# Twelve-stage perceiver decoder: weight-load commands, barriers and small preparations at the seams between stages

## What is computed

```python
x = x + L0_xattn(ln(x), ctx)         # joint attention over own and context tokens
x = x + L0_attn(ln(x))               # self attention, decay, gate
x = x + L0_ffn(ln(x))                # 8 experts, top 2, and a shared one
x = x + L1_xattn(ln(x), ctx, mask)   # 6 decoder layers: self, cross, MLP, each with a norm behind it
x = x + L1_attn(ln(x))
x = x + L1_ffn(ln(x))                # 8 experts, top 2
x = x + L2_xattn(ctx, ctx, ln(x), mask)   # attention at sampled positions
x = x + L2_attn(ln(x))               # cos and sin features (Fourier)
x = x + L2_ffn(ln(x))                # silu(gate) * up, then down; int weights times 1/127
x = x + L3_xattn(ln(x), ctx)
x = x + L3_attn(ln(x))               # gated recurrence
x = x + L3_ffn(ln(x))                # self attention, softplus(temperature) in the queries
return x
```

## Time and profile before

| | |
|---|---|
| median of three runs | 4102.86 us |
| the profiled execution: its own time | 4100.83 us |
| its span, first to last instruction | 4099.0 us |
| mean granted TensorE clock | 0.943 |
| busy: PE, DVE, ACT, POOL | 90%, 63%, 43%, 20% |
| decoder stage, first to last instruction | 690.9 to 2561.2 us |
| DMA | 334.49 MB, mean 82 GB/s |

### The profile page before, as it was taken

How to read it: one execution, slowest core, us unless ns; L and a number is a source line. 1 busy time by engine, 2 the same in 40 slices (tenths; PEclk the granted TensorE clock), 3 DMA queues, 4 the chain that set the end, 5 groups by cost and what they waited for, 6 DMA issues and landing times. The chain is left out here.

```text
span 4099.0 us, 98863 instructions
## 1 busy us (share of the span) xinstructions
PE 3673.6 (90%) x40620; PEld 2808.6 (69%) x40620; DVE 2571.7 (63%) x5495; ACT 1757.3 (43%) x4869; POOL 821.9 (20%) x1040
## 2 busy tenths in 40 slices
PE   7997996999999999999999998759689979888766
PEld 5775985677777777777777776548556679555435
DVE  4445213688888888888888885641168857355545
ACT  1221321444445444444444444312167736266523
POOL 1111101222222222222222222120121100012200
PEclk9998998999999999999999999869889979999877
DMA  4222486001101111101111100227655410010001
GB/s 170 94 81 76 159 301 221 32 32 44 63 32 44 63 33 54 53 33 54 53 38 49 58 28 2 62 86 280 241 185 179 156 37 1 28 42 22 12 7 57
DMA packets 141790, 334.49 MB, mean 82 GB/s; under 512 B 31320, under 2 KB 92184, under 8 KB 122912
## 3 DMA queue, kind: packets, MB, share of 16 engines
q1 hardware_dynamic: 138272, 319.76, 22.9%
q0 software_dynamic: 3072, 8.39, 0.6%
HBM read 301.62 MB, written 26.48 MB: 80 GB/s over the span
## 5 line engine op out<-in xcount | busy, mean ns | idle before, releaser
L2613 POOL TENSOR_TENSOR layers_probs<-layers_probs,layers_rates 128x512 f32<-128x512 f32 x384 | 399.9, 1063 | 867.7 <-DVE layers_rates L2536 867.7
L2640 ACT COPY layers_pT<-banks 128x512 f32<-128x512 f32 x384 | 226.1, 589 | 478.8 <-PE banks L2441 478.8
L2676 ACT ACTIVATE layers_probs<-banks,layers_negmax 128x256 f32<-128x256 f32 x768 | 354.4, 478 | 85.2 <-DVE layers_negmax L2528 85.2
L2370 PE MATMUL banks<-ctx_tiles,weights_a 128*128 128x512 f32 x768 | 364.3, 597 | 0.0
L2377 PE MATMUL banks<-weights_a,ctx_tiles 128*128 128x256 f32 x1536 | 363.1, 379 | 0.0
L2377 PEld LDWEIGHTS banks<-weights_a,ctx_tiles 128*128 128x128 f32 x1536 | 284.6, 190 | 75.9 <-issue 46.1
L2441 PE MATMUL banks<-const,layers_probs 128*128 128x128 f32 x1536 | 243.8, 282 | 3.0 <-POOL layers_probs L2613 3.0
L2441 PEld LDWEIGHTS banks<-const,layers_probs 128*128 128x128 f32 x1536 | 172.3, 142 | 106.6 <-issue 78.6
L2527 DVE TENSOR_REDUCE layers_negmax<-banks 128x4 f32<-128x1024 f32 x192 | 233.7, 1217 | 4.1 <-PE banks L2434 1.6
L2502 DVE COPY layers_V<-banks 128x512 f32<-128x512 f32 x192 | 132.4, 690 | 107.7 <-PE banks L2377 97.7
L2653 ACT ACTIVATE layers_KT<-banks,layers_key_bias 128x512 f32<-128x512 f32 x192 | 133.1, 693 | 155.0 <-PE banks L2370 154.8
(11 more groups left out here) (703 smaller groups left out, 8152.5 us busy)
## 6 DMA issues: line engine op xcount, KB each, us to landing
ctx_tiles<-ctx_rel SPq DMA_DIRECT2D x56, 1024.0 KB, 5.5
weights_a<-in_L_w SPq DMA_DIRECT2D x46, 1024.0 KB, 5.4
l2x_B<-positions SPq DMA_DIRECT2D x32, 1280.0 KB, 6.0
weights_b<-in_L_w SPq DMA_DIRECT2D x32, 1024.0 KB, 6.2
weights_c<-in_L_w SPq DMA_DIRECT2D x16, 1024.0 KB, 7.1
weights_b<-in_L_xattn_w SPq DMA_DIRECT2D x12, 1024.0 KB, 7.4
ctx_tiles<-in_ctx SPq DMA_DIRECT2D x8, 1028.0 KB, 5.7
l0x_key_rows<-in_ctx_rows SPq DMA_DIRECT2D x32, 256.0 KB, 2.7
```

Source lines behind the costliest of these rows:

```text
L2370: last = mm(o, ca_wk[:, c, m * P:(m + 1) * P], E.ctx[:, tile % 2, c, 2 * i * KW:2 * (i + 1) * KW], start=c == 0, stop=c == DC - 1)
L2613: nc.gpsimd.tensor_tensor(probs[:, cc, j // 2, at], probs[:, cc, j // 2, at], rates[:, cc, j // 2, at].unsqueeze(2).to_broadcast([P, 2, KW ...
L2640: nc.scalar.copy(pT[:, k % 4].rearrange("p t c x -> p (t c x)"), o).then_inc(s["evac_act"], 1)
L2676: a(probs[:, cc, j // 2, r], ps[:, r, 0:KW], ACT.Exp, bias=negmax[:, cc, j // 2, r:r + 1], accum_out=totals[:, cc, j // 2, r:r + 1]).then_ ...
```

## The change

1. `end_round` can leave its barrier out. It does so where `await_weights` follows directly: at the end of all twelve stages (after l3f, where the program ends). The small Blocks that stay (`fill` of "proj", `prepare_decay`, `feature_major`, `prepare_centred`) keep theirs.
2. `await_weights` takes several names with one barrier; three pairs are joined.
3. `send_for` moves from the seam into SP's program of the next Block, as `begin` (first thing in l0a, l1a, Fourier and the gated MLP; after step 1 in the decoder; in l2x after the first seven key loads).
4. The fill Blocks of `floor` and `half_pi` go: the one memset moves into `prepare_decay`, the other into the first fill.
5. The decoder's sum goes from one instruction behind the stage to one a tile, behind the last layer's norm.
6. The integer weights are turned in six pieces of 128x768 on DVE inside the Fourier stage, after `mask(k)` at r = 2 of tiles 2 to 7. Their loads are issued at the start of that stage.
7. Softplus moves into `prepare_centred`, on DVE and ACT, ahead of what waits for PE there, with one table load instead of two.
8. The output is stored by eight DMAs of 128 KB at the end of l3f, each when its tile's sum is done.

```diff
-def end_round(nc, handles):
+def end_round(nc, handles, barrier=True):
...
-    nc.all_engine_barrier(sem_only=True)
+    if barrier:
+        nc.all_engine_barrier(sem_only=True)
...
-def await_weights(E, name):
+def await_weights(E, *names):
-    sem, n = E.loads[name]
-    E.nc.sync.wait_ge(sem, 16 * n)
-    E.nc.sync.sem_clear(sem)
+    for name in names:
+        sem, n = E.loads[name]
+        E.nc.sync.wait_ge(sem, 16 * n)
+        E.nc.sync.sem_clear(sem)
     E.nc.all_engine_barrier(sem_only=True)
...
-                        link(v.tensor_tensor(E.x[:, GB * i + g], E.x[:, GB * i + g], y, ALU.add))
+                        v.tensor_tensor(E.x[:, GB * i + g], E.x[:, GB * i + g], y, ALU.add).then_inc(s["x_done"], 1)
...
             def _(sp):
+                if begin:
+                    begin()
                 for g in range(NG):
...
+                if out is not None:
+                    for g in range(NG):
+                        sp.wait_ge(s["x_done"], g + 1)
+                        sp.dma_start(out[:, g], E.x[:, g]).then_inc(s["out_stored"], 16)
+                    sp.wait_ge(s["out_stored"], 16 * NG)
...
                         sp.dma_start(E.ctx[:, step % 2, :, 0:GB * KW], E.ctx_rel[step % NG]).then_inc(s[f"ctx{step % 2}"], 16)
+                    if step == 1:
+                        begin()
...
                     v.tensor_tensor(E.h[:, tile], y, LN_ROWS[kind][:, 2], ALU.add).then_inc(s["h_" + kind], 1)
+                    if kind == "dm":
+                        summed[0] += 1
+                        if summed[0] > (NL - 1) * NG:
+                            dve.wait_ge(s["h_dm"], summed[0])
+                            link(v.tensor_tensor(E.x[:, tile], E.x[:, tile], E.h[:, tile], ALU.add))
...
-                nc.vector.tensor_tensor(E.x[:], E.x[:], E.h[:], ALU.add).then_inc(t["added"], 1)
...
+                v.scalar_tensor_tensor(a[:], E.col("temperature"), -1.0, E.col("temperature"), ALU.mult, ALU.max).then_inc(s["abs"], 1)
+                link(v.tensor_scalar(softplus[:], E.col("temperature"), 0.0, None, ALU.max))
+                dve.wait_ge(s["ln"], 1)
+                link(v.tensor_tensor(softplus[:], softplus[:], a[:], ALU.add))
                 dve.wait_ge(s["done"], 1)
...
                     sp.wait_ge(s["job_done"], number["KV", (K - 4, 1)] + 1)
                     load_ctx(K)
+                begin()
                 for it in range(T):
...
+                def dequantise(piece):
+                    if piece == 0:
+                        sem, n = E.loads[ints_name]
+                        dve.wait_ge(sem, 16 * n)
+                    dst, src = ints[piece // 2]
+                    half = src.shape[1] // 2
+                    at = slice(piece % 2 * half, (piece % 2 + 1) * half)
+                    v.tensor_scalar(dst[:, at], src[:, at], float(np.float32(1.0 / 127.0)), None, ALU.mult).then_inc(s["dequantised"], 1)
...
+                    if r == 2 and g >= 2:
+                        dequantise(g - 2)
...
-        await_weights(E, "L0x")
-        await_weights(E, "L0a")
+        await_weights(E, "L0x", "L0a")
...
-        await_weights(E, "L0f")
-        await_weights(E, "later")
+        await_weights(E, "L0f", "later")
...
-        await_weights(E, "layer0")
-        await_weights(E, "layer0_ca")
+        await_weights(E, "layer0", "layer0_ca")
...
-        send_for(E, "out", [(A["out"].rearrange("(g p) d -> p g d", p=P), E.x[:])])
-        await_weights(E, "out")
```

More of the change, by code:

```diff
@@ L613, in _ @@
                         copy_turned(it - 2)
-        end_round(nc, handles)
+        end_round(nc, handles, barrier=False)
 def context_attention(E, tag, wq, wk, wv, wo, rows, bq, bk, norm, last_v):
@@ L1515, in feature_major, with mlp_block @@
         end_round(nc, handles)
-def mlp_block(E, s, bufs, nT, steps, chunks, func, glu=False, loads=(), norm=None):
+def mlp_block(E, s, bufs, nT, steps, chunks, func, glu=False, loads=(), norm=None, begin=None):
     nc, ps = E.nc, E.ps
@@ L2130, in _ @@
                     normalise(norm_to, E.x, [NG - 1])
-        end_round(nc, handles + [E.scattered] + E.gathered)
+        end_round(nc, handles + [E.scattered] + E.gathered, barrier=False)
 class LayerBuffers:
@@ L2725, in _ @@
             def _(dve):
+                nc.vector.memset(E.layer.floor[:], -10000.0).then_inc(s["floor"], 1)
+                dve.wait_ge(s["floor"], 1)
                 dve.wait_ge(s["sig"], 1)
@@ L3517, in _, with gated_mlp @@
                 take_oT(NG - 1)
-        end_round(nc, handles)
-def gated_mlp(E, w_ints, up, down):
+        end_round(nc, handles, barrier=False)
+def gated_mlp(E, up, down, begin):
     nc = E.nc
@@ L3531, in gated_mlp @@
         sil = st.enter_context(nc.sbuf_tensor("glu_sil", [P, 2, NG * P // 2], F32))
[L3532 to L3539 removed]
         feature_major(E, "glut", nT)
         steps = [{"up": up, "down": down, "half": half, "into": E.x, "weight": lambda g: 1.0} for half in range(2)]
[L3542 to L3543 removed]
+        mlp_block(E, s, (hid, sil), nT, steps, HC, None, glu=True, begin=begin)
+        end_round(nc, handles, barrier=False)
 def gated_recurrence(E, w, rows):
```

129 lines of the change are left out of this document (51 added, 78 removed).

## The result

| | before | after |
|---|---|---|
| median of one comparison on the same chip, us | 4107.6 (4 runs, 4101.1 to 4112.5) | 4070.8 (4 runs, 4063.3 to 4075.9) |
| ratio, 95% interval | | 0.9922 (0.9905 to 0.9939) |
| a second comparison | 4101.8 (9 runs, 4093.6 to 4110.5) | 4067.1 (5 runs, 4063.8 to 4070.6) |
| ratio, 95% interval | | 0.9920 (0.9906 to 0.9934) |
| profiled execution: own time, span | 4100.83, 4099.0 | 4075.89, 4074.1 |

The change makes the kernel 0.8% faster. Against the median of before that the forecast started from, 4102.86, the after median is 32.0 us lower; within its own comparison it is 36.8 lower. The two profiled executions lie only 24.9 apart, less than the seams alone gained. That difference is the thread of what follows.

The account below looks back on a forecast made before the run. Between stages only barriers, small Blocks and load commands run, so that time was taken to lie on the whole kernel's path. Terms sum to 36.9 us, from the median 4102.86 to 4066.0; own range 4059 to 4073, overall 4052 to 4080.

Parts of the forecast that it names:

- Plain barriers: Seams where only barriers are dropped: seven barriers at 0.36 us each, a gain of 2.5 us.
- l0x to l0a: Seam from l0x to l0a: the Block for `floor` and two barriers go, a gain of 2.6 us.
- Fourier: Seam from l2x to Fourier: 7.82 us falls to a bare seam of 1.03, a gain of 6.8 us.
- gated MLP: Seam from Fourier to the gated MLP: 9.44 us falls to 1.03, a gain of 8.4 us.
- l3f: Seam from the recurrence to l3f: 5.70 us, softplus Block included, falls to 1.03, a gain of 4.7 us.
- the end: After the last sum: 6.0 us falls to 2.1 with only the last 128 KB store awaited, a gain of 3.9 us.
- l1f to l2x: Seam from l1f to l2x: the mask is issued 2.8 us earlier and lands in 2.4, a gain of 5.5 us.
- End of the decoder: Seam into l1a gains 2.9 us, tile 6's sum costs 0.46, six other sums nothing: a net gain of 2.5.
- The bad end: Decoder's last layer: if none of the other six sums were covered, they would cost 6 x 0.46 = 2.8 us.
- Covers that held: Six weight pieces inside Fourier and five loads inside l2x: each taken as 0, at worst 2.9 and 2.3 us.
- softplus in `prepare_centred`: In `prepare_centred`, softplus fits into DVE's 4.45 us idle before its first product: cost 0, at worst 1.3 us.
- The rival that the clock gives more: At the four long seams, TensorE stays longer at 2.4 GHz, giving 12.7 us more, 4053 in all; chance 0.12.

Follow-up runs that it names:

- bars_only: The kernel before with one barrier less at eight `end_round` places and three pairs of load waits merged, nothing else moved; 4098.01 us against 4102.19 of before.
- undo_ends: The changed kernel with the decoder's sum again one Block behind the decoder and the output again one store; 4064.71 us.
- better: The changed kernel with the decoder's sums moved into l1a and l2x's first norm ahead of the mask's sums; median 4065.42 us.
- warm: The kernel of better plus 20 TensorE products with unread results, 12 at the decoder's end and 8 at l1a's start; median 4062.98 us.
- after_timed: The changed kernel with no edit, timed in the same rounds as better; median 4067.07 us.
- again_before: The kernel before run once more with no edit; 4090.11 us in one execution.
- blocks_back: The changed kernel with the small Blocks and the weights' turning put back between stages, load commands staying inside the stages; 4079.88 us.
- again_after: The changed kernel run once more with no edit; 4069.33 us in one execution.
- delay5: The changed kernel with five VectorE memsets ahead of each of l1a, the gated MLP's norms and l3f; 4076.87 us.
- delay3: The changed kernel with three VectorE memsets ahead of each of l1a, the gated MLP's norms and l3f; 4064.09 us.
- loads_at_seams: The changed kernel with all moved load commands back between the stages, nothing else; 4066.14 us.

## Why the prediction held, and where it did not

The forecast was 4066.0, the result 4070.8 and 4067.1. Both lie in the forecast's own range of 4059 to 4073.

- *Plain barriers, l0x to l0a, Fourier, gated MLP, l3f, the end*: 28.9 forecast, 29.1 measured. The 0.36 of a barrier holds (0.35 to 0.54 in bars_only), and a bare seam of 1.03 was 0.97 to 1.15.
- *l1f to l2x*: 5.5 forecast, 6.2 measured, the upper end. The mask's landing was put at 2.4 and took 1.7 (2974.09 to 2975.81), the value of the nearest row.
- *End of the decoder*: the seam was right (2.9, measured 3.0), the term was not. "The other six fall where the decoder is bound by PE, and I take nothing for them" is the step that failed: seven sums lengthened the last layer by 3.3 us, where 0.46 was in the forecast. TensorE's busy share says that it has work, not that no part of it waits for DVE. The bad end given, 2.8 for the six, has nearly the right size (2.7 in after) by luck: it took each at its full 0.46, and measured are 0.25 for each of the first four, nothing for the fifth, 1.7 for the sixth; the seventh, of tile 6, cost 0.65.
- *Covers that held*: the six pieces in Fourier cost nothing; the five loads in l2x neither (l2x was 331.0 to 333.6 before, 330.1 to 332.7 in three profiles of after). *One that held less well*: softplus in `prepare_centred`. Its table load was over before DVE's first product, as forecast, but the next stage gained nothing: from the gated MLP's last sum to l3x's first norm it is 6.98 in the three profiles of after, 6.91 before and 6.54 in bars_only, which drops the same barrier and leaves softplus alone. So it cost 0.4 here (0.1 in undo_ends, better and warm, with 6.63).
- *The end*: 3.9 forecast, 3.6 measured. The landing was right: the last 128 KB took 1.7 from the start of the command to SP's next step (4061.53 to 4063.24 in after_timed). Too small was the 0.3 for what follows it: from there to the end of the span it is 0.7. By the Trainium skill's "DMA: Bandwidth & Descriptors", Anatomy of one DMA, the estimate was a landing of 2.3 and a term of 3.3; the measured landings are shorter, 1.7 for the last and 2.0 for the median of the eight. The eight small stores win against its advice to coalesce, 2.4 against 5.2 behind the last sum, as only one of them is waited for.
- *"The twelve stages themselves are not touched"*: wrong for their time. By my own mark (a stage that grows by more than 3 us) the prediction erred at l1a, 7.3 longer in the first profile and 4 to 7.4 in three, and in the first pair also at the decoder (4.4) and the recurrence (3.8; 75.9 before, but 79.6 in again_before and 77.9 to 79.7 after, so this one is scatter). `mlp_block` gave back 1.6 to 1.9 in each profile of after, since it now starts while the clock is still at 1.2 GHz. l3f was 1.9 to 6.6 shorter in three profiles of after, but 107.2 to 108.3 behind the same seam in warm, blocks_back and undo_ends, no shorter than again_before's 107.3. The other two marks held: the mask landed in 1.7, and the mean clock went from 0.943 to 0.945 in the first pair.
- *The rival that the clock gives more* had the sign wrong for `mlp_block` and, in these profiles, for l1a. A TensorE that stays busy does keep its clock (warm shows it), but a seam of 1 us with norm and transposes behind it does not spare TensorE the fall: in every profile with such a seam in front of l1a, the gated MLP or l3f, and no products in it, the clock is at 1.2 GHz when TensorE starts again. It only moves the stage's start against it. The rule of the Trainium skill, in "TensorE: Matmul & The Clock Gate", HAM oscillation, that work behind an idle gap starts cold, is what the earlier trace rows and the windows of `mlp_block` show. Overlooked was that a shorter gap can meet more of the slow stretch than a longer one (again_after against before), and a longer one more than a shorter (delay5 against delay3).

Summed over the first pair of profiles, a plus being shorter: seams +38.3, the decoder's sums -3.3 with another -1.1 in its length, l1a -7.3, mlp_block -1.9, l3f +6.4, the recurrence -3.8, l0a -2.6, the others together +0.2: 24.9, and the two spans lie 24.9 apart. The forecast's total was nearer to the medians than its parts deserved, as l1f's gain above forecast made up for part of the decoder's; that the stages' own ups and downs did not move the medians further is luck, as the forecast had no term for them.

What stays open: whether l1a is longer on the average behind a short seam. Behind the seam of after it took 114.1, 114.0, 114.0, 110.8 and 109.2, behind the seam of before 106.7, 106.8, 106.5 and 110.8 (undo_ends). Without undo_ends the two sets would stand apart; with it they don't, and delay3 and delay5 don't follow the seam's length either. What sets the start of each slow stretch against the stage's own work I could not control.

## What to carry to other kernels

A load command on the queue of an engine costs nothing until somebody waits for that engine: look for the barriers, Blocks and first inputs that stand behind it, and move either the commands or the Block. Work put into a pipelined stage ahead of a result that another engine waits for can be on the path, however busy that engine looks (here half of it in four steps, none in one, more than all of it in the last two together); put it behind the result, or into a stage whose waits are visible. When a few microseconds are taken out between stages, compare the stages too, in more than one profile: their own clock can return or take away as much as the seam gave.

## What the hardware showed that I had not expected

- A stage with the same instructions took 106.5 to 114.1 us, by how much of it ran at 1.2 GHz, in executions whose whole times differ by a few tenths of a per cent. Equal values in two executions (114.1 and 114.0) did not mean that the third would be equal (110.8).
- A deliberate delay of 2.0 us in front of the gated MLP cost nothing (73.3 us with it, 73.2 without), while one of 3.3 cost 3.6: the first let the block start at 2.4 GHz, the second did not.
- Load commands that stand in a row can get longer: 0.38 to 0.47 for the five in front of l2x, but 0.54 to 0.75 from the fourth on in front of Fourier, and 1.72 for the eighth (loads_at_seams). Among the thirteen in front of the gated MLP it is the ninth that takes 0.99, and the tenth 0.47 again. A memset of 512 columns on VectorE takes 0.485, and 0.17 to the next that waits for it.
